# Expert 0's one-hot rows in 16 bits, and the first quarter of w2 behind the stores

## The reference

```python
x = x + jnp.tanh(g_xattn[0]) * _L0_xattn_ref(8, 256, 512, time_decay, time_first, _layernorm(x, axis=-1), ctx_2048)
x = x + jnp.tanh(g_ffn[0]) * _L0_ffn_ref(_layernorm(x, axis=-1), Wg, bg, W1, W2)

def _L0_ffn_ref(x, Wg, bg, W1, W2):
    # E = 4, H = 2048, TOPK = 2, N = 2048, capacity = 512
    logits = flat_x @ Wg + bg
    top_vals, top_idx = jax.lax.top_k(logits, TOPK)
    ...
    probs = jax.nn.softmax(sparse, axis=-1)
    for i in range(E):
        assigned = (top_idx == i).any(axis=-1)
        score = jnp.where(assigned, probs[:, i], -jnp.inf)
        sel_p, sel_idx = jax.lax.top_k(score, capacity)
        p = jnp.where(jnp.isfinite(sel_p), sel_p, 0.0)[:, None]
        tok = flat_x[sel_idx]
        h = jax.nn.gelu(tok @ W1[i], approximate=False)
        y = h @ W2[i] * p
        out = out.at[sel_idx].add(y)
```

## Time and profile before

| | us |
|---|---|
| median of 3 runs | 463.74 (463.54 to 463.96) |
| the profiled execution | 463.81 |
| its span | 461.8 |

### The profile page before, as it was taken

The page is one execution under the profiler, slowest core; times in us unless marked ns, Lnnn a source line. Parts: engine busy times, 40 slices in busy tenths (PEclk is TensorE's granted clock), DMA queues, the critical chain, the costliest instruction groups (busy, mean ns, idle before and its releaser), DMA issues.

```text
span 461.8 us, 7153 instructions
## 1 busy us (share of the span) xinstructions
PE 412.7 (89%) x2067; PEld 203.9 (44%) x2067; DVE 284.7 (62%) x582; ACT 313.2 (68%) x491; POOL 112.2 (24%) x130
## 2 busy tenths in 40 slices
PE   2589898533999999999999999999999999999992
PEld 1444454211844444444444444444444444444472
DVE  7999899898599966655753192456517445550010
ACT  6799899998588783847778780777879057760000
POOL 0788766603100003620003221100132110001121
PEclk9999999955899999999999999999999999999997
DMA  7975120698401746895003959300195510001212
GB/s 257 367 319 229 45 92 1 251 343 278 153 1 50 315 170 217 164 246 206 0 0 126 350 86 320 120 0 1 46 380 114 73 24 0 0 0 14 33 23 24
DMA packets 36327, 62.80 MB, mean 136 GB/s; under 512 B 14352, under 2 KB 14736, under 8 KB 34256
## 3 DMA queue, kind: packets, MB, share of 16 engines
q1 hardware_dynamic: 32064, 53.32, 33.3%
q0 software_dynamic: 3808, 8.65, 9.4%
q10 hardware_dynamic: 432, 0.54, 0.3%
HBM read 46.78 MB, written 12.58 MB: 129 GB/s over the span
## 4 chain that ended last, share of the span: by engine, by line
PE 76%; DVE 7%; issue 2%; POOL 1%; ACT 1%; DVEq 0%; POOLq 0%
PE ps L877 34%; PE ps L862 27%; PE ps L842 7%; PE ps L805 2%; PE ps L890 2%; DVE arena L1388 1%; DVE arena L1659 1%; PE ps L668 1%; POOL arena L1231 1%; PE ps L625 1%; DVE arena L1419 1%; DVE arena L1786 0%; PE ps L797 0%; PE ps L645 0%; PE ps L614 0%
## 5 line engine op out<-in xcount | busy, mean ns | idle before, releaser
L877 PE MATMUL ps<-arena 128*128 128x512 f16 x720 | 156.5, 379 | 0.0
L862 PE MATMUL ps<-arena,early 128*128 128x512 f16 x576 | 124.8, 379 | 0.0
L877 PEld LDWEIGHTS ps<-arena 128*128 128x128 f16 x720 | 69.9, 98 | 83.6
L862 PEld LDWEIGHTS ps<-arena,early 128*128 x576 | 56.4, 98 | 67.9
L1128 ACT ACTIVATE arena<-ps,up 128x512 f32<-128x512 f32 x64 | 43.8, 684 | 58.2 <-PE ps L862 40.8
L1838 DVE SCALAR_TENSOR_TENSOR arena<-arena,h_down 128x512 f32 x48 | 36.1, 751 | 58.5 <-ACT arena L1131 58.5
L1309 POOL DMA_INDIRECT result<-arena,idx x15 | 27.7, 1847 | 175.3 <-DVE arena L1866 113.8
L1131 ACT ACTIVATE arena<-arena,h_down 128x512 f32 x64 | 46.2, 722 | 8.7 <-ACT arena L1128 0.2
L1817 DVE SCALAR_TENSOR_TENSOR early<-w_raw,down,early 128x2048 f16<-128x2048 f32 x16 | 37.0, 2346 | 18.8 <-ACT early L1085 18.8
L1134 ACT ACTIVATE arena<-rows,down x64 | 45.2, 706 | 0.0
L1866 DVE TENSOR_SCALAR arena<-ps,yscale 128x512 f32<-128x512 f32 x15 | 11.2, 747 | 50.6 <-PE ps L877 39.3
(11 more groups left out here) (238 smaller groups left out, 479.9 us busy)
## 6 DMA issues: line engine op xcount, KB each, us to landing
w_raw<-in_L_ffn_W SPq DMA_DIRECT2D x4, 4096.0 KB, 14.1
rows<-in_L_ffn_W SPq DMA_DIRECT2D x3, 4096.0 KB, 17.6
rows<-in_L_ffn_W SPq DMA_DIRECT2D x4, 1024.0 KB, 9.2
result<-rows SPq DMA_DIRECT2D x3, 1024.0 KB, 8.6
early<-in_ctx SPq DMA_DIRECT2D x2, 1024.0 KB, 6.5
rows<-in_x SPq DMA_DIRECT2D x2, 1024.0 KB, 11.6
xn_table<-arena SPq DMA_DIRECT2D x4, 512.0 KB, 5.7
xn_table<-arena SPq DMA_DIRECT2D x2, 1024.0 KB, 5.2
```

What stands on the lines that cost most here:

```text
L862: last = nc.tensor.matmul(ps[:, PH[q], :], w[:, k, at], t[:, k, :], start=n == 0, stop=n == 3 * CT - 1)
L877: last = nc.tensor.matmul(ps[:, PY[s % 2], :], h[:, t, s * P:(s + 1) * P], w[:, t, :], start=t == 0 and n == 0, stop=t == HT - 1 and n == 2)
```

## The change

Three things are edited. The one-hot rows of expert 0 are built from 16-bit numbers: a table of slot numbers (`slot_numbers`, 16-bit, 512 KB over all partitions) is loaded behind the stores into the part of `arena` where the high half of w2 will lie later, and the compare writes `hot_0` with the tile index innermost, so the 16 list products read their weights with a step. `put` of expert 0 comes from four compare-and-multiply instructions, one for each of the four tiles of slots, in place of the product `in_a` and one multiplication. Quarter 0 of w2 is issued behind the last stores. And the norms of tiles 0 and 1 move from units 8 and 9 to 11 and 12.

```diff
-NORMS2 = {8: (0,), 9: (1,), 14: (2,), 15: (3,), 16: (4,), 17: (5,), 18: (6,), 19: (7,)}
+NORMS2 = {11: (0,), 12: (1,), 14: (2,), 15: (3,), 16: (4,), 17: (5,), 18: (6,), 19: (7,)}
...
-    return t
+    slots = np.ascontiguousarray(np.broadcast_to(np.repeat(np.arange(P, dtype=np.int16), TT)[None], (P, P * TT)))
+    return np.ascontiguousarray(np.concatenate([t, slots.view(np.float32)], 1))
...
+        hot_0 = part(arena, [at[0]], (P, TT), F16)
         hot = part(arena, at, (TT, P), F16)
+        slot_numbers = part(arena, [HT * D // 2], (P, TT), I16)
...
             for g in range(NG - 2):
                 store_x1(g)
                 store_xn2(g)
-            first_w2(0, (0, 1))
             store_x1(NG - 2)
             store_x1(NG - 1)
             store_xn2(NG - 2)
             store_xn2(NG - 1)
+            sp.wait_ge(s_scan, UNITS)
+            sp.dma_start(arena[:, HT * D // 2:HT * D // 2 + C_SLOTS], consts[:, C_ALL:]).then_inc(s_id, 16)
+            first_w2(0, (0, 1))
             first_w2(1, (2,))
             first_w2(2, (3,))
...
-                last = nc.tensor.matmul(ps[:, PI, 0:ST * 4], hot[:, t, :], put[:, 0, t, :], start=t == 0, stop=t == TT - 1)
+                last = nc.tensor.matmul(ps[:, PI, 0:ST * 4], hot_0[:, :, t], put[:, 0, t, :], start=t == 0, stop=t == TT - 1)
...
-            step(nc.vector.scalar_tensor_tensor(posi[:, 0, :], pos[:, 0, 0, :], FAR, pos[:, 1, 0, :], ALU.add, ALU.add))
-            nc.vector.tensor_scalar(slot_b[:, 0, :], posi[:, 0, :], P - 1, None, ALU.bitwise_and).then_inc(b_dve, 1)
-            step(nc.vector.tensor_scalar(slot_a[:, 0, :], posi[:, 0, :], 7, None, ALU.logical_shift_right), 2)
-            step(nc.vector.tensor_tensor(in_a[:, 0, :, :], slot_a[:, 0, :].unsqueeze(2).to_broadcast([P, TT, ST]),
-                                         cst[:, C_IOTA:C_IOTA + ST].unsqueeze(1).to_broadcast([P, TT, ST]), ALU.is_equal))
+            step(nc.vector.scalar_tensor_tensor(posi_0[:, :], pos[:, 0, 0, :], FAR, pos[:, 1, 0, :], ALU.add, ALU.add))
+            nc.vector.tensor_scalar(slot_b0[:, :], posi_0[:, :], P - 1, None, ALU.bitwise_and).then_inc(b_dve, 1)
+            step(nc.vector.tensor_scalar(slot_a0[:, :], posi_0[:, :], 7, None, ALU.logical_shift_right), 2)
...
+                if isinstance(e, int) and e == 0:
+                    for a in range(ST):
+                        nc.vector.scalar_tensor_tensor(put[:, 0, :, 4 * a:4 * a + 4],
+                                                       slot_a0[:, :].unsqueeze(2).to_broadcast([P, TT, 4]), float(a),
+                                                       vals[:, 0], ALU.is_equal, ALU.mult)
...
+                    if isinstance(e, int) and e == 0:
+                        dve.wait_ge(s_id, 32)
+                        nc.vector.tensor_tensor(hot_0[:, :, half], slot_numbers[:, :, half],
+                                                slot_b0[:, half].unsqueeze(1).to_broadcast([P, P, TT // 2]),
+                                                ALU.is_equal).then_inc(b_hot, 1)
+                        continue
```

More of the change, by code:

```diff
@@ L58 @@
 I32 = mybir.dt.int32
+I16 = mybir.dt.int16
 U32 = mybir.dt.uint32
@@ L68 @@
 C_ALL = C_NEXT0 + EXACT0
+C_SLOTS = P * TT // 2
 S_TD, S_GATE, S_WG, S_BG = 0, 2 * CT, 2 * CT + 2, 2 * CT + 2 + CT * E
@@ L193, in part @@
             cols = math.prod(dims)
-            words = cols * (2 if dt in (F16, BF16) else 4) // 4
+            words = cols * (2 if dt in (F16, BF16, I16) else 4) // 4
             v = home[:, at[0]:at[0] + words]
@@ L301, in program @@
         posi = sb("posi", [P, E, TT], I32)
+        posi_0 = sb("posi_0", [P, TT], I16)
+        slot_a0 = sb("slot_a0", [P, TT], I16)
+        slot_b0 = sb("slot_b0", [P, TT], I16)
         slot_a = sb("slot_a", [P, E, TT], I32)
@@ L527, in _ @@
             sp.dma_start(c_sb[:, a:b, :], rows_of(c_v, a, b)).then_inc(s_c[1], 16)
-            sp.dma_start(cst[:, C_TRI:], consts[:, C_TRI:]).then_inc(s_cst, 16)
+            sp.dma_start(cst[:, C_TRI:], consts[:, C_TRI:C_ALL]).then_inc(s_cst, 16)
             a, b = FIRST[2], FIRST[3]
@@ L1777, in slots @@
             def slots(e):
-                nc.vector.tensor_tensor(put[:, e, :, :].rearrange("p t (a c) -> p t a c", a=ST),
-                                        in_a[:, e].unsqueeze(3).to_broadcast([P, TT, ST, 4]),
-                                        vals[:, e].unsqueeze(2).to_broadcast([P, TT, ST, 4]), ALU.mult)
+                if isinstance(e, int) and e == 0:
[3 more added lines that the diff above has]
+                                                       vals[:, 0], ALU.is_equal, ALU.mult)
+                else:
+                    nc.vector.tensor_tensor(put[:, e, :, :].rearrange("p t (a c) -> p t a c", a=ST),
+                                            in_a[:, e].unsqueeze(3).to_broadcast([P, TT, ST, 4]),
+                                            vals[:, e].unsqueeze(2).to_broadcast([P, TT, ST, 4]), ALU.mult)
                 if e >= 1:
@@ L1996 @@
     arrays["in_constants"] = constant_table()
-    args.append(nc.dram_tensor("in_constants", (P, C_ALL), F32, kind="ExternalInput").ap())
+    args.append(nc.dram_tensor("in_constants", (P, C_ALL + C_SLOTS), F32, kind="ExternalInput").ap())
     args.append(nc.dram_tensor("result", (BATCH, SEQ, D), F32, kind="ExternalOutput").ap())
```

## The result

The changed kernel takes 471.65 us, median of 4 runs (471.04 to 471.75), and the kernel before beside it 463.85 (463.54 to 465.01, 4 runs). The ratio is 1.0161, with a 95% interval from 1.0141 to 1.018: slower. The prediction said 469.3, with a range from 466.9 to 471.4. The direction and the mechanism hold; the time is 2.4 us later than forecast and 0.25 us outside the range. The profiled execution took 471.75, its span is 469.8, 8.0 more than before.

The account below looks back on a forecast made before the run. Bound: TensorE's stream, where any shift of the first feed-forward product (118.59) reaches the end whole. Late quarter 0 +5.7, norms -0.1, 16-bit rows 0: +5.6 on 463.81, 469.4, as a median 469.3; range 466.9 to 471.4.

Parts of the forecast that it names:

- the mechanism: ScalarE's sum over late quarter 0 holds w1's casts, ending at 118.5, not 112.45; first product 5.7 us later.
- From the casts' end to the first product: TensorE's warm-up twice, transposes and ScalarE's copy take 5.8 us, not 6.14; the 0.35 wait between warm-up groups goes.
- I take 108.8: Landing of quarter 0 of w2, issued at about 102.0 behind the xn2 stores and slot numbers: 108.8 us.
- the late bound of 110.2: Latest landing allowed for quarter 0: 110.2 us, where quarter 1 landed in the kernel before.
- the late clock: Rival at TensorE's first product: full clock only after the first 16 products, +1.9 more, 471.2 us; chance 0.10.
- By bytes: Quarter 0's landing: same bytes as landed by 106.8 plus 0.5 MB at 3.4 us a megabyte, 108.5.
- By steps: Quarter 0's landing: first xn2 store 103.9, second 1.3 later, slot numbers 1.3 more, quarter 0 2.6 more: 109.1.
- Its own cover: Slack for the slot numbers in expert 0's list: landing above 106.5, wanted at 108, inside a 5 us cover.
- I take 0: Expert 0's two compares on VectorE, 2.28 us together, gain nothing from 16-bit operands; at best -1.8.
- Overtaking: Rival in the DMA queue: quarter 0 passes the xn2 stores, lands at 106.9; +3.8, or 467.4 with norms; chance 0.06.
- The other side: Rival: ScalarE gets quarter 0 in time, compares take half; 1.1 us and the norms' 0.1 gained, 462.6; chance 0.04.

Follow-up runs that it names:

- late-only kernel: Kernel before with only quarter 0 of w2 issued behind the last xn2 store, no slot load, 16-bit rows or moved norms: 470.87 us, ratio 1.0155.
- the swapped one: Changed kernel with ScalarE's four casts of w1 put ahead of its sum over quarter 0, transfers unchanged: 466.45 us, ratio 1.0065 against the kernel before.
- both loads early: Changed kernel with the slot numbers and quarter 0 both issued ahead of the last x1 stores: 462.95 us, ratio 0.9979 against the kernel before.
- the earlier warm-up: Changed kernel with slot numbers and quarter 0 ahead of the last x1 stores, first warm-up waiting only for w1's first cast: 463.23 us, ratio 0.9988.

## Why the prediction was right, and where its size was off

**The mechanism: right.** ScalarE waits in program order for quarter 0 ahead of w1's casts; TensorE waits for the casts; the stream behind passes the delay on whole. All of it is in the rows above. The late-only kernel shows that this edit makes nearly all of it, the one with quarter 0 back in place that the rest of the change costs no time on balance, and the swapped one that the order on ScalarE passes it on.

**From the casts' end to the first product: right.** 5.8 us was the term; 120.82 to 126.55 is 5.73. The 0.35 between the two warm-up groups went, as said.

**The landing: mis-sized, and with it the sum.** The step that failed is "I take 108.8", the landing of quarter 0. It measured 111.07, 2.27 later, and behind the late bound of 110.2 too; that is the whole miss of 2.35 us but for 0.1. From there to the casts' end (120.82) it is 9.75, where the step had 9.7. That the time still ended within 0.25 us of the range is luck: the upper end, 471.4, was set for the late clock, which did not come. Both ways to the landing fell:

- *By bytes*, 108.5. It took the queue to carry the same megabytes in the same time in another order. But the queue was dry from 98 to nearly 100, because the stores that follow must wait for their data. Taking a transfer out of a gap that nothing else can fill gives no time back.
- *By steps*, 109.1. The first xn2 store landed at 103.95 (forecast 103.9). Then the second took 2.3 more where 1.3 was forecast, the slot numbers 1.72 where 1.3 was, and quarter 0 3.1 where 2.6 was: 1.97 in all, to 111.07. The pace of 2.6 us a megabyte was the mean of 99.0 to 106.8 in the kernel before, about 400 GB/s up to 104 and 247 from 104 to 106. In the new order the fast part is mostly gone and the slow one is left. Why the queue slows there stays open: with both loads early the same stores pass at 400.

The nearest row was at hand, and I used it as the outer bound: quarter 1 stood directly behind the same xn2 stores and took 8.7. Put behind the issue at 101.5 to 102.8, it gives 110.2 to 111.5, which holds what was measured in every kernel with a late quarter 0 (109.9 to 111.5) but for 0.3. The bound itself was wrong in its working: 110.2 was the landing of a quarter issued at 101.49, and this one went out at 102.77, not at the 102.0 of the prediction, since issuing the slot load took SyncE 1.21 us.

**The slot load: its part stays open.** The sum by steps held it as 1.3 us ahead of quarter 0. The two kernels with nothing between the stores and quarter 0 put it at 0.2 and 1.2. Its own cover held: it landed at 107.97, 1.5 later than forecast, and the compares started at 108.04. That is level with it, so nothing was left of this cover; in the kernel with quarter 0 back in place the compares did wait for it, 0.29 us.

**The 16-bit compares: "I take 0" was wrong, and didn't matter.** VectorE's groups from 107 to 111 us (busy, mean ns, then idle), in the kernel after:

```profile
L1802 DVE TENSOR_TENSOR arena<-arena,slot_b 128x1024 f16<-128x1024 int16 x2 | 1.3, 688 | 0.0
...
L772 PEld LDWEIGHTS ps<-put,arena 128*128 128x128 f16 x16 | 1.2, 163 | 2.8 <-DVE arena L1802 2.7
```

A compare takes 688 ns, not the 1216 of before. The four that build `put` need 0.61 from start to start of the next, where two instructions had 0.68. The list products load their weights with a stride now, the only thing that was changed in them: 163 ns a load, where the packed ones took 105. The sum is 0.8: `idx` at 110.09, not 110.90. The Trainium skill's rule in "VectorE: DVE Perf Modes", section "What auto-detection actually checks", which I set against the row of `put`, held: the estimate of 1.2 for the two that I worked out from it stands beside 1.29 measured. `put` was the wrong neighbour, as one of its operands repeats each element (an innermost step of 0), which those of the compare do not. The cover held too, so none of it reaches the changed kernel's time.

**The rivals.** Overtaking: no, quarter 0 landed behind both xn2 stores in all five kernels that issue it behind them. The clock late: not in the changed kernel. Its windows from 126.5 on:

```profile
126.50:127.00 0.50, 0.45 (x4) 0.40 (x5) 0.50 (x1) 0.50 (x2) 0.00 (x0) 0.76 0.00 0
127.00:128.00 1.00, 1.00 (x12) 0.90 (x10) 0.73 (x2) 1.00 (x1) 0.00 (x0) 1.00 0.00 0
```

The rise from the lower to the full clock fell at the first product, and its 16 products took 1.98, where the late-only kernel's took 1.91. The other side: no; the kernel with both loads early, where the load is in time, comes near to its 462.6 (462.95), but by luck. The 1.1 us were to come from the compares, and the four casts, which still end near 112.3, don't allow that; what came instead was the wait between the warm-up groups and a clock that rose earlier.

## What to carry to other kernels

Before moving a load back in an in-order queue, find the first instruction that waits for it in an in-order engine's program and everything queued behind that instruction; that queue, not the load's use, sets the price. Take the landing from the row of a transfer that stands in the same place behind the same neighbours, not from bytes over a pace: a gap that only this load could fill is lost when it leaves. Where a stage becomes faster under cover of another, look at the next arrival (here quarter 3) before counting the gain.

## What the runs showed of the hardware

- A megabyte load behind 1.5 MB of stores takes 8.3 to 9.5 us in all five kernels with a late quarter 0, for 5.4 on a quiet queue, and the quarters behind it are at most 0.7 of that. Windows with full DMA engines (share 1.05 to 1.07) went at 206 GB/s in the changed kernel and at 410 in the one before.
- Token gathers took 3.7 us before (median of four) and 5.1 (casts first) to 5.7 (the changed kernel) when quarters of w2 were in flight at the time; with the quarters held back until quarter 0 had landed, up to 7.1.
- A compare of 16-bit operands, one of them repeated along the outer axis, runs at 688 ns per 1024 elements, against 1216 for 32-bit ones. Loading 128x128 16-bit weights whose columns stand 32 bytes apart took 163 ns, packed ones 105, both at the lower clock.
- One 1.89 us copy on GpSimd held a 0.24 us VectorE instruction for 1.44.
- TensorE's clock (granted 0.50, 1.2 GHz, up to there) rose to 1.00 (2.4 GHz) at the first product in the changed kernel, where warm-ups and transposes without a gap above 0.34 us follow an idle stretch of 8.99. In the casts-first kernel, with gaps of 1.6 and 0.3 us among them, it had not risen there yet. With quarter 0 back in place it rose before the transposes (1.00 from 115 us), with both loads early during them, and with the earlier warm-up only between 117 and 118. What decides was not tried.
